# Row biases of the attention scores by two small transfers in place of one-column products

## The reference

```
x = x + cross_attention(norm(x), ctx, ctx)     # q, k, v seen as (tokens / 2, 16 heads, 64)
x = x + selective_scan_block(norm(x))          # 1024 inner channels, 16 states, conv of 4 taps
x = x + mixture_of_experts(norm(x))            # 16 experts, 4 of them per token
```

## Time and profile before

| | us |
|---|---|
| median of 3 runs | 1369.88 |
| lowest, highest | 1369.01, 1376.7 |
| the profiled execution | 1377.52 |
| its span | 1375.8 |
| PE busy | 1176.5 (86%) |
| DVE busy | 881.7 (64%) |
| ACT busy | 631.7 (46%) |
| POOL busy | 134.1 (10%) |

### The profile page before, as it was taken

One profiled execution on the slowest core, in us unless ns is written; L12 is line 12 of the kernel. 1 busy time (PEld: TensorE's weight loads), 2 busy tenths in 40 slices (PEclk: granted clock), 3 DMA queues, 4 the chain that ended last, 5 costly groups with the idle time before them and its releaser, 6 DMA issues.

```text
span 1375.8 us, 13572 instructions
## 1 busy us (share of the span) xinstructions
PE 1176.5 (86%) x4404; PEld 757.3 (55%) x4404; DVE 881.7 (64%) x946; ACT 631.7 (46%) x1398; POOL 134.1 (10%) x113
## 2 busy tenths in 40 slices
PE   5996869777897899999789999935999999999993
PEld 4884736555464557667456766533454445545451
DVE  1121376875657789995878998585999993323312
ACT  4452565445247466736555663642545441223221
POOL 0010001311000007000001600021000000223102
PEclk9897988999899799999889999957999998999997
DMA  7256101999630025540003523018899993999993
GB/s 272 77 169 251 40 16 43 388 401 358 213 127 8 9 70 160 150 144 15 14 10 107 168 60 140 9 61 297 317 380 358 363 374 111 371 354 408 409 397 123
DMA packets 114037, 266.22 MB, mean 194 GB/s; under 512 B 10160, under 2 KB 43056, under 8 KB 113968
## 3 DMA queue, kind: packets, MB, share of 16 engines
q1 hardware_dynamic: 98096, 207.16, 43.2%
q0 software_dynamic: 15872, 58.20, 10.8%
HBM read 197.03 MB, written 68.29 MB: 193 GB/s over the span
## 4 chain that ended last, share of the span: by engine, by line
PE 50%; DVE 29%; DMA 9%; ACT 8%; issue 3%; POOL 1%; SPq 0%; POOLq 0%; DVEq 0%; ACTq 0%
DVE state L1350 10%; PE bank L811 8%; PE bank L679 7%; PE bank L772 7%; PE bank L691 5%; DVE state L1347 5%; PE bank L832 4%; PE bank L712 4%; DMA ctx<-in_ctx_t 4%; DVE state L1357 2%; DVE y_acc L1361 2%; DVE decay L1354 2%; ACT decay L1104 2%; PE bank L616 2%; PE bank L646 2%
## 5 line engine op out<-in xcount | busy, mean ns | idle before, releaser
L1350 DVE TENSOR_TENSOR_SCAN state<-decay,state 128x2048 f32<-128x2048 f32 x64 | 283.0, 4421 | 40.2 <-ACT decay L1104 39.4
L811 PE MATMUL bank<-expert_w,block_x_t 128*128 128x512 f32 x496 | 227.4, 602 | 1.8 <-ACT block_x_t L1156 1.7
L679 PE MATMUL bank<-decay,params 128*128 128x512 f32 x384 | 183.5, 624 | 4.3 <-DVE decay L1354 4.3
L1104 ACT ACTIVATE decay<-delta_even,params 128x256 f32<-128x256 f32 x256 | 107.2, 496 | 103.7 <-PE bank L679 95.2
L1641 POOL DMA_INDIRECT dispatched<-ffn_x,slot x32 | 73.0, 2281 | 779.0 <-DVE slot L1443 770.5
L811 PEld LDWEIGHTS bank<-expert_w,block_x_t 128*128 128x128 f32 x496 | 91.8, 195 | 93.9 <-issue 91.9
L691 PE MATMUL bank<-ctx,queries_ctx 128*128 128x256 f32 x512 | 120.8, 392 | 19.7 <-DMA ctx<-in_ctx_t 18.5
L712 PE MATMUL bank<-probs,ctx 128*128 128x256 f32 x512 | 121.9, 393 | 11.6 <-ACT probs L1013 6.9
L1104 ACT ACTIVATE decay<-delta_odd,params 128x256 f32<-128x256 f32 x256 | 106.2, 499 | 43.6 <-PE bank L679 34.0
L679 PEld LDWEIGHTS bank<-decay,params 128*128 128x128 f32 x384 | 75.5, 200 | 84.7 <-issue 78.0
L712 PEld LDWEIGHTS bank<-probs,ctx 128*128 128x128 f32 x512 | 100.9, 198 | 36.4 <-issue 14.9
(11 more groups left out here) (196 smaller groups left out, 1398.9 us busy)
## 6 DMA issues: line engine op xcount, KB each, us to landing
dispatched<-ffn_x POOLq DMA_DIRECT2D x38, 1024.0 KB, 25.0
expert_w<-in_eg_t SPq DMA_DIRECT2D x62, 512.0 KB
expert_w<-in_eu_t SPq DMA_DIRECT2D x62, 512.0 KB
expert_w<-in_ed_t SPq DMA_DIRECT2D x62, 512.0 KB, 9.7
ctx<-in_ctx_t SPq DMA_DIRECT2D x32, 512.0 KB, 6.9
ctx<-in_ctx_n SPq DMA_DIRECT2D x32, 512.0 KB, 4.3
bc_bcast<-bc_scratch SPq DMA_DIRECT2D x64, 256.0 KB, 6.0
block_x<-dispatched SPq DMA_DIRECT2D x62, 256.0 KB
```

The lines of the kernel that those rows point to most:

```text
L679: mm = pe.matmul(y_bank[c][:, :], ident, dA[(g * NS + j) % NDEC][:, c * 512:(c + 1) * 512], start=False, stop=(j == NS - 1))
L811: mm = pe.matmul(o, xbT[q % 2][:, c, :], w_gu[q % NW][:, :, c, :], start=(c == 0), stop=(c == DC - 1))
L1104: ins = act.activation(dA[n % NDEC][:, k * gt:(k + 1) * gt], dlt[g][:, k, :], ACT.Exp, scale=par[:, c:c + 1])
L1350: dve.tensor_tensor_scan(h, dA[n % NDEC][:, 0:sw], h, 0.0, ALU.mult, ALU.add).then_inc(scan_rd, 1)
```

## The change

The key bias is copied once, from PSUM to `kb`, 8 partitions by 256, in the order (token, unit) within a head. SP stores it to memory (8 rows of 1 KB), waits for the store, and loads it as 128 partitions by 2 blocks by 8 units, pieces of 32 bytes, into `rowb_`. The 16 one-column products (L665), ACT's copy of them (L967) and the seven further key-bias copies are gone. `neg_max` of unit 0 waits for the load (`rowb_in`) in the same place. In SP's order the step `spread_key_bias(g + 1)` stands after the second of the four `load_bc` ahead of group g+1's units, that is after `load_bc(g * 16 + 3)`; for group 0 it stands behind the load of the output weights, the last of the start-up. `kb` lies in the first columns of the buffer of the probabilities. The wait for the previous store of B and C moves from `key_bias` to `proj_bc`.

```diff
--- before.py
+++ after.py
@@ -127,7 +127,7 @@
         out += [("q", g)] * DC + [("key_bias", g)]
         if g >= 2:
             out += [("ffn_norm", g - 2)] * NTS[g - 2] + [("logits", g - 2)]
-        out += [("query_ctx", g)] * (DC * DC // 4) + [("row_bias", g)] + [("query_ctx", g)] * (DC * DC // 4)
+        out += [("query_ctx", g)] * (DC * DC // 2)
         for k in range(NUS[g] + 1):
             if k >= 1:
                 out += [("wctx", UNIT0[g] + k - 1)] * 2
@@ -163,7 +163,6 @@
         xs = xs_[:, :].rearrange("p (n d) -> p n d", d=D)
         nrm_ = sb("normed", 2 * NT * D)
         nrm = nrm_[:, :].rearrange("p (n d) -> p n d", d=D)
-        sb8 = [nrm_[0:H, 0:NUS[g] * Q].rearrange("p (u h i) -> p u h i", u=NUS[g], h=H) for g in range(NGR)]
         bcT = [nrm_[0:2 * NS, 0:GTS[g]] for g in range(NGR)]
         fx_ = sb("ffn_x", NT * D)
         fx = fx_[:, :].rearrange("p (n d) -> p n d", d=D)
@@ -206,7 +205,7 @@
         nmax = sb("neg_max", 2 * QB)
         rsum = sb("row_sum", 2 * QB)
         rowb_ = sb("row_bias", 2 * NU * QB)
-        rowb = [rowb_[:, g % 2 * NU * QB:(g % 2 + 1) * NU * QB] for g in range(NGR)]
+        rowb = [rowb_[:, g % 2 * NU * QB:g % 2 * NU * QB + NUS[g] * QB].rearrange("p (b u) -> p u b", b=QB) for g in range(NGR)]
         ones8 = sb("ones", 1)
         epsc = sb("eps", 1)
 
@@ -220,6 +219,7 @@
             pp_ = sb("probs", 4 * QB * KEYS, stack=early)
             prob = [pp_[:, s * 512:(s + 1) * 512].rearrange("p (b k) -> p b k", b=QB) for s in range(2)]
             probT = [pp_[:, 1024 + s * 512:1536 + s * 512].rearrange("p (j q) -> p j q", j=KC) for s in range(2)]
+            kb = [pp_[0:H, 0:GTS[g]] for g in range(NGR)]
             XP = 2 * GB * (T + TAPS - 1)
             xi = [[pp_[:, s * XP:s * XP + 2 * n * (T + TAPS - 1)].rearrange("p (k t) -> p k t", t=T + TAPS - 1)
                    for s in range(2)] for n in GBS]
@@ -270,6 +270,7 @@
             return v[:, 1024:1024 + DC * GTS[c]].rearrange("p (c t) -> p c t", c=DC)
 
 
+        kb_dram = nc.dram_tensor("key_bias_rows", (NGR, QB, H // QB * TI, NU), F32, kind="Internal").ap()
         xd = [nc.dram_tensor(f"dispatched_{w}", (ROWS[w], D), F32, kind="Internal").ap() for w in range(len(WAVES))]
         yd = [nc.dram_tensor(f"expert_out_{w}", (BLOCKS[w] * P, D), F32, kind="Internal").ap() for w in range(len(WAVES))]
 
@@ -316,8 +317,9 @@
         a_free = sem("bankA_free")
         d_full = sem("bankD_full")
         d_free = sem("bankD_free")
-        sb8_rdy = sem("qbk_ready")
-        rowb_rdy = sem("row_bias_ready")
+        kb_rdy = sem("key_bias_ready")
+        kb_out = sem("key_bias_written")
+        rowb_in = sem("row_bias_in")
         q_full = sem("ctx_queries_full")
         q_free = sem("ctx_queries_copied")
         s_full = sem("scores_full")
@@ -417,6 +419,17 @@
                 sp.dma_start(bcs[k % 2][:, 0:2 * GTS[g]].rearrange("p (w t) -> p w t", w=2),
                              src.unsqueeze(0).to_broadcast([P, 2, GTS[g]])).then_inc(bc_in[k % 2], 16)
 
+            def spread_key_bias(g):
+
+                sp.wait_ge(kb_rdy, g + 1)
+                rows = kb_dram[g].rearrange("b r u -> b (r u)")[:, 0:H // QB * GTS[g]]
+                sp.dma_start(rows.rearrange("b (h t) -> (b h) t", h=H // QB), kb[g]).then_inc(kb_out, 16)
+                sp.wait_ge(kb_out, 16 * (g + 1))
+                if g >= 2:
+                    sp.wait_ge(nm_rdy, UNIT0[g - 1])
+                sp.dma_start(rowb_[:, g % 2 * NU * QB:g % 2 * NU * QB + NUS[g] * QB].rearrange("p (b u) -> p b u", b=QB),
+                             rows.rearrange("b (p u) -> p b u", p=P)).then_inc(rowb_in, 16)
+
             def expert_of(w, j):
 
                 sp.wait_ge(tab_rdy, w + 1)
@@ -475,6 +488,7 @@
             sp.dma_start(bcw, bc_t.rearrange("(c p) e -> p c e", p=P)).then_inc(sw_in, 16)
             sp.dma_start(gwt, gate_t.rearrange("(c p) e -> p c e", p=P)).then_inc(sw_in, 16)
             sp.dma_start(ow, ow_t.rearrange("(k p) d -> p k d", p=P)).then_inc(ow_in, 16)
+            spread_key_bias(0)
             for n in range(1, NUS[0] + 1):
                 load_ctx_t(n + 1)
                 load_ctx_n(n)
@@ -486,6 +500,8 @@
 
                 for s in range(LEAD):
                     load_bc(g * NS + s + 2)
+                    if s == 1:
+                        spread_key_bias(g + 1)
                 for k in range(NUS[g + 1]):
                     n = UNIT0[g + 1] + k + 1
                     load_ctx_t(n + 1)
@@ -649,22 +665,10 @@
                                     mm.then_inc(a_full, 1)
                         if mp == 0:
                             mm.then_inc(q_full, 1)
-                    if c == 1:
-                        row_bias(g)
                     if g > 0 and c in (1, 2, 3):
                         sum_state(g - 1, c - 1)
                 pe.wait_ge(q_free, (g + 1) * QPAIRS)
                 pe.wait_ge(a_free, ja.n)
-
-            def row_bias(g):
-
-                pe.wait_ge(sb8_rdy, g + 1)
-                b = job_a()
-                for k in range(NUS[g]):
-                    for qb in range(QB):
-                        mm = pe.matmul(b[:, k * QB + qb:k * QB + qb + 1], sb8[g][:, k, qb * 4:(qb + 1) * 4, :], ones8[0:H, :],
-                                       start=True, stop=True)
-                mm.then_inc(a_full, 1)
 
             def start_sum(g):
 
@@ -962,11 +966,6 @@
                                 ins.then_inc(a_free, 1)
                         if mp == 0:
                             ins.then_inc(q_free, 1)
-                    if c == 1:
-                        b = job_a()
-                        act.activation(rowb[g][:, 0:NUS[g] * QB], b[:, 0:NUS[g] * QB], ACT.Copy).then_inc(a_free, 1)
-                        act.wait_ge(a_free, ja.n)
-                        act.nop().then_inc(rowb_rdy, 1)
                     if lead:
                         scan_decay(g - 1, lead.pop(0))
                 assert not lead
@@ -975,13 +974,10 @@
 
                 b = job_a()
                 if g:
-                    act.wait_ge(bc_out, 16 * g)
-                for h in range(H):
-                    ins = act.activation(sb8[g][:, :, h, :], b[0:H, 0:GTS[g]].rearrange("p (u i) -> p u i", u=NUS[g]),
-                                         ACT.Copy, scale=ident[0:H, h:h + 1])
-                ins.then_inc(a_free, 1)
+                    act.wait_ge(kb_out, 16 * g)
+                act.activation(kb[g].rearrange("p (i u) -> p u i", u=NUS[g]), b[0:H, 0:GTS[g]].rearrange("p (u i) -> p u i", u=NUS[g]), ACT.Copy).then_inc(a_free, 1)
                 act.wait_ge(a_free, ja.n)
-                act.nop().then_inc(sb8_rdy, 1)
+                act.nop().then_inc(kb_rdy, 1)
 
             def exps(n):
                 act.wait_ge(nm_rdy, n + 1)
@@ -1021,6 +1017,8 @@
 
             def proj_bc(g):
                 b = job_a()
+                if g:
+                    act.wait_ge(bc_out, 16 * g)
                 act.activation(bcT[g], b[0:2 * NS, 0:GTS[g]], ACT.Copy).then_inc(a_free, 1)
                 act.wait_ge(a_free, ja.n)
                 act.nop().then_inc(bc_rdy, 1)
@@ -1281,11 +1279,11 @@
 
                 n = UNIT0[g] + k
                 nm = nmax[:, n % 2 * QB:(n % 2 + 1) * QB]
-                add = rowb[g][:, k * QB:(k + 1) * QB]
+                add = rowb[g][:, k, :]
                 dve.wait_ge(s_full, n + 1)
                 step(dve.tensor_reduce(nm, bank[n % 2][:, :].rearrange("p (b k) -> p b k", b=QB), AX_X, ALU.max, negate=True))
                 if k == 0:
-                    dve.wait_ge(rowb_rdy, g + 1)
+                    dve.wait_ge(rowb_in, 16 * (g + 1))
                 step(dve.tensor_tensor(nm, nm, add, ALU.subtract))
                 dve.tensor_tensor(nm, nm, add, ALU.add).then_inc(nm_rdy, 1)
```

## The result

The changed kernel takes 1338.2 us, median of four runs (1334.18 to 1341.93), against 1372.45 for the kernel before beside it (1369.01 to 1376.7). The ratio is 0.975, 95% interval 0.970 to 0.980, a gain of 34 us. The forecast was 1330, with a range of 1321 to 1346. Of the 8 us between forecast and median 2.6 come from the median of before (1369.9 in the prediction, 1372.45 here) and 5.7 from the gain (40.0 forecast, 34.3 measured). The profiled execution of the changed kernel took 1334.18 (span 1332.2), 43 us less than the profiled one of before.

What follows compares the result with a forecast made beforehand. The bound changes by stage; in the four preparations PE's products stall ACT and, through it, DVE. Gains of 12.0 + 10.3 + 8.1 + 9.6 = 40.0 us from 1369.9 give 1330 us, range 1321 to 1346.

Steps and rivals of the forecast that it cites:

- A: Only what is removed is gained, 24.0 us of products and 2 of copies: 1344 us; chance 0.13.
- B: Transfers amid the clears keep group 1's end where it is, so 10.3 us is lost: 1340 us; chance 0.10.
- Group 0: Preparation before the first scores: they start at 35.9 in place of 48.14 us; gain 12.0, low bound 7.6.
- the choice of full clock: In group 0's preparation PE runs at full clock, left no gap over 1 us; at the 1.2 GHz level gain 7.6.
- Group 1: Its preparation: neg_max at 226.0 in place of 236.26 us, DVE late next; gain 10.3, bounds 6.2 and 11.7.
- the first neg_max of groups 2 and 3: Ends of preparation: 493.1 in place of 498.57 us (gain 5.5), and 721.4 in place of 728.14 (6.7).
- The waits for positions: In groups 2 and 3, DVE's waits of 2.75 and 3.64 us shrink after the first neg_max: 2.6 and 2.9 gained.
- DVE's wait closes: gain 8.1: Group 2: positions come 8.1 us earlier, so DVE's 2.75 us wait for them goes; bounds 5.5 and 9.5.
- Gain 9.6: Group 3: DVE's 3.64 us wait for positions shrinks with a chain moved by 9.6 us; bounds 6.7 and 10.8.
- The round trip: Store and load of the bias take 12 us (8 to 20), hidden before neg_max; at 20 group 0 loses 6.
- Rival C: Row bias comes late, DVE waits before L1289; over 1% slower from 42.5 us (chance 0.04), within 1% from 34 (0.05).
- The price of the products: PE's one-column products cost 0.19 us per instruction, weight load included, 24.0 us over 128.

Runs made afterwards that it cites:

- four kernels with narrow and wide products: The changed kernel with products of zeros in groups 1 to 3, one-column or 512-column, before the first scores or after the second round: 1343.9, 1349.5, 1345.04, 1349.66 us.
- early narrow: The changed kernel with 16 one-column products of zeros after the second round of queries_ctx in groups 1 to 3: 1345.04 us, ratio 0.980.

## Why the prediction was right

The time fell into the range, and the mechanism was the one forecast: PE's wait at the products and what stood behind it. The gain is another matter. The prediction's own band for it was 34 to 49 us, with rivals A and B below, and 34.3 lies at its edge. By the total alone B (30 us) can't be told from it, since the interval of the ratio allows 28 to 41; it is the stretches that decide.

**Point by point.** *Group 0*, 12.0 forecast, 12.1 measured: the choice of full clock was right. The reason is now better than the one I gave. I took the clock to stay up because no gap over 1 us was left; the four kernels with narrow and wide products show that the products alone can lower it, without a gap. The Trainium skill (TensorE: Matmul & The Clock Gate, Part 1: The HAM clock gate) puts the clock down to how busy TensorE has been; the trace agrees for the 3.99 us gap, but not for the one-column products: PE's rows show it busy for 3.50 of 3.50 us in them (early narrow, group 1), and the clock fell behind them. The eight copies were 3.8 of the 12.

*Group 1*, 10.3 and 10.8, and *the first neg_max of groups 2 and 3*, 5.5 and 6.7 against 5.2 and 6.8: right in size and in who is late next. Here 16.4 of 22.8 us came from the wait for the bank and what followed from it, the clock already low in the products among it; 6.4 came from the products and the clock behind them, of which only 0.1 in the group where that clock stayed up.

*The waits for positions*, mis-sized. The step was "DVE's wait closes: gain 8.1", and "Gain 9.6" in group 3. The term was 2.6 and 2.9 on top of the first `neg_max`; it measured 1.1 and 1.1. ACT's normalising came about where I had it: counted from group 1's x add it moved from 135.0 to 127.0 us, 8.0 earlier (forecast 8.3), in group 3 by 9.5 (9.6). But the positions stand one round of scores further on, and moved 6.3 and 7.8. The difference is 1.7 each time, the 5.31 in place of 3.62 us of these scores. What the prediction left out is that PE, further ahead than before, stands idle for 3.99 us there and the clock falls; it took these scores as unchanged without a reason given. At group 3's end the context product (L716 at 769.4) took 5.41 in place of 3.72, behind an idle 1.93 us that stood there before too. That is not shown to be the change's doing: the end of a group had either length, 28.4 or 26.7 us, in kernels with and without it (28.4 in group 2 of before). The two are 3.3 and 1.7 us of what the gain lacks to 40.0, in the one profile; small gains elsewhere stand against them. The low end of the range had PE's own gains in it; in the first `neg_max` of groups 1 to 3 they could not show, as DVE was late there.

*The round trip*, 12 us forecast with bounds of 8 and 20, measured 4.8 in group 0 (26.38 to 31.2) and 5.4 in group 1. The nearest rows were of 32 and 256 KB; the load landed in 1.7 us. It cost nothing either way, since 14 us were free. The warning of the Trainium skill (DMA: Bandwidth & Descriptors, Specifications), that transfers below 512 B are off line rate, does not decide here: 256 pieces of 32 B were landed 1.7 us after the issue. Rival C needed a trip of 34 us and more.

*The price of the products*, 0.19 us per instruction from the row: it is the mean over two clocks. It measured 0.11 at full clock (3.51 over 32; 3.73 with the kernel's own products, placed last, in group 2) and 0.19 at a mean clock of 0.57 (6.18 over 32). The sum did not depend on it in groups 1 to 3, as it was made from the ends of waits.

*The two executions.* I subtracted the gain of one profiled execution from a median 7.6 us lower, without knowing that the group 1 stretch has two lengths 4 to 8 us apart. The profile of before was one with the long length, as were seven others. The medians hide it; a comparison of single profiles would have given 43 us for a change that is worth 34.

**What stays open.** That a load issued up to 1.5 us behind the start of nine clears is hardly waited for, and one issued 3 us or more behind is, was seen in eleven profiles but not tried by moving that load alone; why is open. So is why the clock fell behind the one-column products in some groups and not in others. The expert phase varied by some 5 us between profiles of kernels that do not differ in it.

## What to carry to other kernels

A small operation in the middle of a pipeline is worth more than its busy time: follow the bank that it needs, the engine that frees that bank, and what stands behind both. A round trip through memory is free where its reader comes later than it lands, and the reader's slack is read from the timeline. When a stage gets shorter, look for an engine that now idles where it did not: its clock may fall and take a part back.

## What the runs showed of the hardware

- One-column float32 products can lower the granted clock of what follows, though PE shows no idle time: 16 of them (3.5 us) were followed by a mean clock of 0.68 and a sum of states of 5.40 us in place of 3.70 in group 1, by scores of 8.85 and 8.86 in place of 7.17 in groups 1 and 2, but by 3.70 and 7.17 in two further places. 512-column products were followed by the fast form in all nine places (7.08 us of them in six, 3.64 us in three).
- PE idle for 3.99 us, the same: the next scores took 5.31 us in place of 3.62. Filled with products of zeros they took 3.62. An idle 2.60 us at this place before was followed by 3.62, an idle 1.93 us before the last context product of group 3 by 3.72 in one kernel and 5.41 in the other.
- A store of 8 KB and a load of 256 pieces of 32 bytes took 4.8 us together on quiet rings, the load 1.7 of it, and 3.0 when repeated at once.
- Nine 1 MB clears from POOL and a 256 KB load from SP: issued 0.8 to 1.5 us after the clears' start, the load cost DVE 0.65 to 2.74 us of waiting; issued 3.0 to 8.9 after it, 5.8 to 9.0 (eleven profiles).
